# Mamba-2 layer on 8 cores: the skip product D·x of each chunk is computed by GpSimd instead of VectorE

## The reference

```python
def step(h, inputs):
    dA_t, dt_t, B_t, x_t, C_t = inputs
    dBx = jnp.einsum('bh,bn,bhp->bhpn', dt_t, B_t, x_t)
    h = h * dA_t[:, :, None, None] + dBx
    y = jnp.einsum('bhpn,bn->bhp', h, C_t)
    return (h, y)
_, ys = jax.lax.scan(step, h0, (tm(dA), tm(dt), tm(Bm), tm(x), tm(Cm)))
y = jnp.moveaxis(ys, 0, 1) + D[None, None, :, None] * x
y = y.reshape(b, l, D_INNER)
y = rmsnorm(y * jax.nn.silu(z), ssm_norm_w)
```

## Time and profile before

| | us |
|---|---|
| three timed runs of the kernel | 4554.42, 4644.46, 4697.14 |
| their median | 4644.46 |
| the profiled execution, its own time | 4551.86 |
| its span on the slowest core (core 2) | 4550.3 |
| spans of the 8 cores | 4526.7 to 4550.3 |

### The profile page before, as it was taken

How to read it: one execution, slowest core, us unless ns; L and a number is a source line. 1 busy time by engine, 2 the same in 40 slices (tenths; PEclk the granted TensorE clock), 3 DMA queues, 4 the chain that set the end, 5 groups by cost and what they waited for, 6 DMA issues and landing times.

```text
span 4550.3 us, 36161 instructions; the slowest of 8 cores (4526.7 to 4550.3 us)
## 1 busy us (share of the span) xinstructions
PE 2233.4 (49%) x9511; PEld 1010.7 (22%) x9681; DVE 1830.4 (40%) x3941; ACT 557.4 (12%) x1011; POOL 82.9 (2%) x136
## 2 busy tenths in 40 slices
PE   0536503337750334343433322777776706877777
PEld 0212201113320111111111111333333302333333
DVE  3532596643139565656565640222222201222222
ACT  3000030000123121212121210111111000000000
POOL 0110000000000000000000000000000000000000
PEclk9998755559975555555555556778888757998988
DMA  5652000011210311111111136000000082111111
GB/s 161 189 155 59 19 0 1 1 40 22 58 54 0 93 56 42 56 45 53 47 52 47 52 73 113 19 19 19 28 19 19 14 154 47 49 33 33 49 33 35
DMA packets 85968, 234.08 MB, mean 51 GB/s; under 512 B 23856, under 2 KB 24656, under 8 KB 85136
## 3 DMA queue, kind: packets, MB, share of 16 engines
q0 software_dynamic: 32128, 106.44, 10.3%
q1 hardware_dynamic: 51344, 116.94, 8.3%
q10 hardware_dynamic: 2304, 8.39, 0.5%
HBM read 235.13 MB, written 51.66 MB: 63 GB/s over the span
## 4 chain that ended last, share of the span: by engine, by line
PE 42%; DVE 21%; issue 16%; DMA 9%; ACT 5%; another core or an unknown queue 5%; DVEq 1%; SPq 0%; ACTq 0%; POOL 0%; POOLq 0%
PE P L1053 4%; PE P L1207 4%; PE P L1203 4%; PE P L1057 3%; PE P L926 3%; PE P L420 3%; PE P L425 3%; DVE Emt L842 3%; DMA wbuf<-w_in 3%; PE PS L1242 2%; DMA bcast<-lam_dram 2%; PE PS L1094 2%; PE P L645 2%; PE P L1242 2%
## 5 line engine op out<-in xcount | busy, mean ns | idle before, releaser
L848 PE MATMUL P<-x_tok,Emt 128*128 128x64 bf16 x512 | 108.3, 212 | 284.7 <-DVE Emt L842 271.3
L549 DVE SCALAR_TENSOR_TENSOR B_acc<-xbc,c_convw,B_acc 128x2048 bf16<-128x2048 bf16 x108 | 245.3, 2345 | 0.0
L1224 DVE TENSOR_TENSOR F_h<-F_h,P 128x1024 bf16<-128x1024 bf16 x48 | 58.6, 1221 | 442.0 <-ACT F_h L1218 442.0
L1203 PE MATMUL P<-wg,F_xf 128*128 128x512 bf16 x368 | 140.0, 381 | 171.6 <-DMA wd2b<-w_d 126.7
L833 ACT ACTIVATE Est<-Est 128x128 f32<-128x128 f32 x512 | 154.8, 308 | 424.2 <-DVE Est L827 422.8
L1074 DVE TENSOR_TENSOR E_h<-E_h,P 128x1024 bf16<-128x1024 bf16 (+1 forms) x48 | 53.3, 1110 | 336.4 <-ACT E_h L1068 336.4
L332 PE MATMUL P<-c_identf,A_n 128*128 128x128 f32 x256 | 90.5, 445 | 197.8 <-DVE A_n L320 166.1
L842 DVE SCALAR_TENSOR_TENSOR Emt<-Est,dtk,Gm 128x128 bf16<-128x128 f32 x512 | 175.8, 346 | 8.4 <-PE P L848 5.2
L1053 PE MATMUL P<-wg,E_hnT 128*128 128x512 bf16 x368 | 139.7, 404 | 66.1 <-ACT E_h L1068 65.6
L434 DVE TENSOR_TENSOR xbc<-P,r1bc 128x1024 bf16<-128x1024 f32 x72 | 88.3, 1227 | 199.5 <-PE P L425 195.1
L827 DVE TENSOR_SCALAR Est<-bcast,lam_tok 128x128 f32<-128x128 f32 x512 | 143.6, 286 | 58.1 <-DMA bcast<-lam_dram 5.8
(11 more groups left out here) (198 smaller groups left out, 4232.6 us busy)
## 6 DMA issues: line engine op xcount, KB each, us to landing
bcast<-lam_dram SPq DMA_DIRECT2D x64, 512.0 KB
A_x<-x_own SPq DMA_DIRECT2D x32, 512.0 KB, 4.2
A_x<-x_pre SPq DMA_DIRECT2D x32, 512.0 KB, 4.1
wd<-w_d POOLq DMA_DIRECT2D x2, 5376.0 KB, 106.6
xn_dram<-A_n POOLq DMA_DIRECT2D x16, 512.0 KB, 5.0
xfh<-xfp_dram SPq DMA_DIRECT2D x4, 2048.0 KB, 14.4
sz_dram<-zst POOLq DMA_DIRECT2D x32, 256.0 KB, 2.3
sz_t<-sz_dram POOLq DMA_DIRECT2D x16, 512.0 KB, 5.1
```

Source lines behind the costliest of these rows:

```text
L549: e.scalar_tensor_tensor(a[:, :], xbc[:, ec * CW + k:ec * CW + k + T], self.c["convw"][:, ec * 4 + k:ec * 4 + k + 1], a[:, :], ALU.mult, A ...
L1203: e.matmul(slots[j][:, 0:512], xft[p][:, dc * 128:(dc + 1) * 128], w[:, dc * INTER2 + cb:dc * INTER2 + cb + 512], start=(dc == 0), stop=(d ...
```

## The change

The product `tD` goes from VectorE's queue to GpSimd's, and counts on GpSimd's semaphore `sg`. Its operands, its type and its waits stay. `ev_y2`, which reads it, waits for `sg` instead of `sv`. The first copy into `x_tok` of the next chunk gets a wait for the product of this chunk, since another engine now reads `x_tok` there. That wait is kept in a dictionary `t_tD`.

```diff
@@ -663,6 +663,7 @@
         t_lch = {-2: 0, -1: 0}
+        t_tD = {}
         pend_tail = {}
@@ -781,7 +782,9 @@
                                    xtra_tr=[("sa", self.t_xbc)] if f == 0 else (),
-                                   xtra_ev=[("st", t_smm)] if f == 0 else ())
+                                   xtra_ev=[("st", t_smm),
+                                            ("sg", t_tD.get(ch - 1))]
+                                   if f == 0 else ())
@@ -855,12 +858,13 @@
-                tD = self.op("vector", lambda e: e.tensor_tensor(
+                tD = self.op("gpsimd", lambda e: e.tensor_tensor(
                     cscr[:, :], x_tok[:, :], c["dexp"][:, :], ALU.mult),
-                    wait=[("sv", t_xtok), ("sa", t_endB[ch - 1][1])], inc=("sv", 1))
+                    wait=[("sv", t_xtok), ("sa", t_endB[ch - 1][1])], inc=("sg", 1))
+                t_tD[ch] = tD
                 ev_y2 = self.op("vector", lambda e: e.tensor_tensor(
                     y_acc[:, :], y_acc[:, :], cscr[:, :], ALU.add),
-                    wait=[("sv", ev_y), ("sv", tD)], inc=("sv", 1))
+                    wait=[("sv", ev_y), ("sg", tD)], inc=("sv", 1))
```

## The result

| | us |
|---|---|
| kernel before, median of 47 runs | 4584.85 (4548.42 to 4787.12) |
| changed kernel, median of 44 runs | 4536.65 (4520.67 to 4773.7) |
| ratio of the two, from undisturbed runs | 0.9944, 95% interval 0.9926 to 0.9962 |
| profiled execution before and after | 4551.86 and 4540.54 |
| spans of the 8 cores after | 4495.8 to 4539.0 |

Some executions of either kernel run up to 5% longer with a lower clock on one die; the ratio leaves them out, and the medians do not. The change made the kernel 0.56% faster. Of the 4551.86 us of the profiled execution that is 25 us. The steps of the forecast came to 26.4.

What follows compares the result with a forecast made beforehand. It took VectorE's chain at each chunk's end, with `tD` on it in all 16 chunks, as the bound; 15 x (-1.87) + 1.62 = -26.4 us from 4551.86 gave 4525, range 4505 to 4650.

Steps and rivals of the forecast that it cites:

- the first chunk: No spill ahead of GpSimd's product there, so `xw` on VectorE waits 3.82 us, more than the 2.20 gained.
- What the removal gives: End of each chunk: `ev_y2` starts 2.39 us after `ev_y` instead of 4.59; 2.20 us a chunk, 35.2 in all.
- The product's duration: `tD` on GpSimd: 4.57 us, twice VectorE's time, chosen between 2.28 and 6.85.
- The hold: Head loop: VectorE's first operation with two SBUF inputs waits for GpSimd's product to end; 0.33 us a chunk; chance 0.58.
- D: The duration of the product `tD` on GpSimd in us, taken as 4.57.
- rival 4: Output product: shorter chunks may move the clock's rise; about 6 us in all, either sign; chance 0.04 shared with anything else.
- Rival 1: Head loop: GpSimd's product doesn't disturb VectorE, so the full 35.2 us is gained, giving 4517; chance 0.18.
- Rival 2: First line 842 of each chunk: product holds VectorE beyond the cover, slower from 6.2 us, 4562 at 6.85; chance 0.16.
- the cover: VectorE's 4.24 us between the product's start and its first operation with two SBUF inputs, where a hold costs nothing.
- Rival 3: Heads 16 to 23: the moved `sz_t` load delays the `bcast` read, losing 42 us in all, giving 4567; chance 0.04.

Runs made afterwards that it cites:

- e4_double: The changed kernel with the product computed twice in a row on GpSimd, the second waiting for the first; ratio to the kernel before 1.0044.
- e5_late: The changed kernel with GpSimd's product waiting for head 8, so that it runs wholly under the head loop; ratio to the kernel before 1.0039.

## Why the prediction was right or wrong

**The number.** The step that failed is "4551.86 - 26.4 = 4525.5, called 4525". It puts the sum on the profiled execution, while the kernel's time was given as a median, 4644.46. Read against that median, 4525 says 2.6% faster, and the measured change is 0.56%. The prediction saw this ("On that scale the same sum gives 4618") and still took the other scale for its one number. 23 of the 47 runs of the kernel before lie below 4575 and the others reach up to 4787, so a median of three says little about the level. What the steps did forecast is a change: -26.4 of 4551.86 is a ratio of 0.9942, and 0.9944 was measured. The range, 4505 to 4650, had to be as wide as the scatter of single runs for this reason, and holds the 4536.65. The error was to state a time where only a ratio could be stated well.

**The mechanism.** That -26.4 comes close is partly luck. The sum was 35.2 - 5.0 (the holds of 15 chunks) - 3.8 (the first chunk). The traces show 34.1 - 7.8 - 0, and a loss of about 3 to 4 us by the clock, which the sum didn't have. The next paragraphs take them one by one.

**What the removal gives.** 2.20 us a chunk was forecast and 2.13 came: the addition behind starts 2.46 us behind its predecessor, not 2.39. Over 16 chunks 34.1 instead of 35.2 us.

**The product's duration.** 4.57 us was chosen between 2.28 and 6.85, and it is 4.06. The 4497 ns that the Trainium skill gives (GPSIMD Engine Reference, Elementwise side-by-side cycle accounting) are for f32 inputs. These are bf16 with an f32 result; whether that makes the difference wasn't tried.

**The hold.** The place was wrong and the size close. The step said: "The first with two SBUF inputs is the first line 842", 4.24 us behind the product's start, so a hold of 0.33 us at 4.57. By that step a product of 4.06 us would have cost nothing. Instead the first exponent, with one tensor input, was held, 3.36 us behind the product's start (1890.58 - 1887.22), and the head loop lost 0.52 us, 7.8 us over 15 chunks. A duration taken too long and a place taken too late partly cancelled. The Trainium skill has the rule that was read only in part (SBUF, Who interferes with whom): an operation of the tensor-scalar kind can also use the shared pair in a two-port mode, when its operands meet that mode's conditions, and whoever issues first keeps it for the whole instruction. The traces agree: 4.14 us for one held line 845, 4.17 for one held exponent, none for operations that read PSUM, and both directions in e4_double. In which mode the exponents run no trace shows, and no run moved an input of a held operation into PSUM; that the place of the inputs decides rests on the kinds of operations seen.

**The first chunk.** 3.82 us was forecast for `xw` at D = 4.57, by D - 0.75. With D = 4.04 the step gives 3.3, and 3.21 was measured. So the hold itself was right. What failed is the path: the sum charged it to the span in full, and the wait of the ninth exponent for `bcast` took it up (5.69 us idle before, 2.56 after). It cost nothing.

**The clock.** 34.1 - 15 x 0.52 = 26.3 us, and the mean scan gave 22.1. Most of the other 4.2 lies in the output product. On core 2 its 15 products behind the first 15 `ev_y` took 8.58 us in the mean before and 8.86 after. How long one takes goes with the clock that it was granted. The shortest of them and the longest, before and after (start and end, us, PE busy, granted clock, DMA share, GB/s):

```profile
2315.12:2323.49 8.37, 8.37 (x32) 0.82 0.00 0
1713.49:1722.30 8.81, 8.81 (x32) 0.78 0.00 0
```

```profile
2223.68:2231.61 7.93, 7.93 (x32) 0.86 0.00 0
1633.21:1642.81 9.60, 9.60 (x32) 0.71 0.00 0
```

Before the change the 15 products had 0.78 to 0.82, after it 0.71 to 0.86 with a lower mean. Over all 8 cores the mean product grew from 8.89 to 9.12 us and its granted clock fell from 0.785 to 0.769, which makes 15 x 0.23 = 3.4 us. This is rival 4, the shift of the point at which the clock rises from 1.2 GHz, with the sign against the change; the prediction had it in the range and not in the sum. That the product slowed with the clock is measured. Why shorter chunks shift the point was not tried.

**The rivals.** Rival 1, no interference, is refuted by the two held operations. (It differs from the forecast by 8.8 us, of which the first chunk is 3.8 and the holds of the others 5.0, so not mainly by the first chunk.) Rival 2 named the mechanism and the break-even: the product would have to last longer than the cover. e5_late takes the cover away instead, and the kernel gets slower by 0.39%, as the rival said of such a hold. Rival 3, the collision of the moved load with a `bcast` read, didn't come: the exponents wait for `bcast` no longer than before, and the load of `sz_t` lands in 4.4 us in the median on core 2 instead of 5.1.

## What to carry to other kernels

Before work is moved from one engine to another, look at where it stands on the path: here leaving it on VectorE, in a stretch where VectorE idles, shortened the scan by 28.0 us against the 22.1 of the change, and a look at its neighbours gave nearly four times as much. Look in the same way at what a delay meets next: 3.2 us lost in the first chunk vanished in a wait for a DMA. When work goes to GpSimd while VectorE computes, list what VectorE does in those microseconds: operations that read PSUM go on, and the first that needs GpSimd's way into SBUF stands still until GpSimd's instruction is over. And forecast a ratio where single runs of one kernel scatter by 3%.

## What I had not expected of the hardware

- A held VectorE instruction shows as a long one (0.97, 4.14 and 5.50 us in place of 0.29, 0.35 and 2.29), not as idle time with a releaser. The column of means hides it where it is one in 32 (303 against 286 ns): look at the longest in the source view.
- An f32 exponent of 128x128 with a per-partition scalar (line 830) is held like an operation with two SBUF tensors, though it takes the usual 286 ns when it is alone.
- GpSimd's product itself is held too when VectorE's operation has the way first: 5.85 us in place of 4.04 in e4_double.
